# Q projection by Strassen's seven products in a transformer layer on one NeuronCore, with the stages reordered through DRAM

## The reference

```python
    x = x + xattn(layernorm(x), ctx, ctx, mask, Wq, Wk, Wv, Wo)
    x = x + ffn(layernorm(x), W_base, b_base, W_router, A, B)
# xattn: x and ctx are (16, 128, 1024); 32 query heads, 8 key/value heads, d = 128
    q = rope((query @ Wq).reshape(b, t, 32, 128));  k = rope((key @ Wk).reshape(b, t, 8, 128))
    v = (value @ Wv).reshape(b, t, 8, 128)
    logits = 30.0 * tanh(q k^T * 0.0883883 / 30.0), masked, then softmax
    return (weights @ v).reshape(b, t, 32 * 128) @ Wo
# ffn: 8 experts, top 2, rank 16
    base = xf @ W_base.T + b_base
    w = softmax of the top 2 router logits, spread over the 8 experts
    lora = einsum('ter,te,eor->to', einsum('td,erd->ter', xf, A), w, B) * 2
```

## Time and profile before

| | before |
|---|---|
| median of 3 runs | 2381.96 us (2380.62 to 2385.32) |
| span of the profiled execution | 2386.6 us |
| busy: PE, DVE, ACT, POOL | 2275.9, 1897.6, 928.1, 1286.0 us |
| matmuls | 9793 |
| moved by DMA | 258.35 MB, mean 108 GB/s |

### The profile page before, as it was taken

How to read it: one execution, slowest core, us unless ns; L and a number is a source line. 1 busy time by engine, 2 the same in 40 slices (tenths; PEclk the granted TensorE clock), 3 DMA queues, 4 the chain that set the end, 5 groups by cost and what they waited for, 6 DMA issues and landing times.

```text
span 2386.6 us, 26853 instructions
## 1 busy us (share of the span) xinstructions
PE 2275.9 (95%) x9793; PEld 1856.3 (78%) x9793; DVE 1897.6 (80%) x1954; ACT 928.1 (39%) x1306; POOL 1286.0 (54%) x720
## 2 busy tenths in 40 slices
PE   8999999999999899999989999998999999888999
PEld 6887878788887678888777888777778887777777
DVE  7436384787889898888998788899888789988992
ACT  3323334343453334334433434444333444333341
POOL 4235454456676445558654445855555476634441
PEclk9999999999999999999999999999999999999999
DMA  7545533232222242222224223222323322133331
GB/s 254 173 155 204 175 119 123 80 93 94 89 97 80 80 159 82 94 96 92 89 80 159 88 89 93 84 83 68 94 88 101 97 80 97 62 124 121 128 102 65
DMA packets 92482, 258.35 MB, mean 108 GB/s; under 512 B 9152, under 2 KB 25664, under 8 KB 92352
## 3 DMA queue, kind: packets, MB, share of 16 engines
q1 hardware_dynamic: 92352, 256.63, 33.0%
HBM read 227.24 MB, written 29.36 MB: 108 GB/s over the span
## 4 chain that ended last, share of the span: by engine, by line
PE 56%; DVE 24%; POOL 10%; issue 8%; ACT 2%; DMA 0%; DVEq 0%; SPq 0%; POOLq 0%; ACTq 0%
PE ps L450 18%; PE ps L451 18%; PE ps L452 18%; DVE AN L752 5%; POOL Rl L270 3%; DVE D L595 3%; POOL t L506 2%; POOL ql L270 2%; DVE Rl L270 2%; DVE L L537 2%; DVE t L503 2%; DVE t L501 1%; DVE Y L788 1%; DVE t L500 1%; POOL D L593 1%
## 5 line engine op out<-in xcount | busy, mean ns | idle before, releaser
L270 POOL TENSOR_TENSOR Rl<-raw,Rh 128x1024 fp32r<-128x1024 f32 x219 | 548.3, 2504 | 607.6 <-ACT Rh L267 606.3
L267 ACT ACTIVATE Rh<-raw 128x1024 fp32r<-128x1024 f32 x360 | 380.0, 1056 | 466.9 <-PE ps L452 457.7
L450 PE MATMUL ps<-Xh,Rh 128*128 128x512 f32 x1296 | 511.5, 395 | 13.3 <-DVE Xl L270 8.1
L450 PE MATMUL ps<-Ah,Rh 128*128 128x512 f32 x1296 | 509.8, 393 | 9.0 <-DVE Al L270 4.8
L451 PE MATMUL ps<-Xl,Rh 128*128 128x512 f32 x1296 | 509.5, 393 | 0.0
L452 PE MATMUL ps<-Xh,Rl 128*128 128x512 f32 x1296 | 508.9, 393 | 0.0
L451 PE MATMUL ps<-Al,Rh 128*128 128x512 f32 x1296 | 508.1, 392 | 0.0
L452 PE MATMUL ps<-Ah,Rl 128*128 128x512 f32 x1296 | 508.1, 392 | 0.0
L752 DVE RECIPROCAL AN<-ps 128x512 f32<-128x512 f32 x128 | 429.0, 3352 | 15.6 <-PE ps L748 12.4
L506 POOL TENSOR_TENSOR t<-t,t 128x512 f32<-128x512 f32 x160 | 251.0, 1569 | 195.4 <-DVE t L503 195.4
L270 DVE TENSOR_TENSOR Rl<-raw,Rh 128x1024 fp32r<-128x1024 f32 x141 | 220.3, 1565 | 101.6 <-ACT Rh L267 100.1
(11 more groups left out here) (139 smaller groups left out, 2960.2 us busy)
## 6 DMA issues: line engine op xcount, KB each, us to landing
raw<-gran SPq DMA_DIRECT2D x361, 512.0 KB, 3.5
raw<-ctxT SPq DMA_DIRECT2D x16, 512.0 KB, 4.3
kD<-t SPq DMA_DIRECT2D x32, 256.0 KB, 3.2
kraw<-kD SPq DMA_DIRECT2D x32, 256.0 KB, 2.6
vD<-st SPq DMA_DIRECT2D x32, 256.0 KB, 2.3
vraw<-vD SPq DMA_DIRECT2D x32, 256.0 KB, 3.2
Y<-xT SPq DMA_DIRECT2D x16, 512.0 KB, 6.6
out<-Y SPq DMA_DIRECT2D x16, 512.0 KB, 2.6
```

Source lines behind the costliest of these rows:

```text
L267: return put("act", waits, lambda e: e.activation(dst, src, ACT.Copy), cn("act_" + name), cost)
L270: return put(eng, waits, lambda e: e.tensor_tensor(dst, src, f(hidst), ALU.subtract), cn(eng + "_" + name), cost)
L450: put("pe", waits, lambda e: e.matmul(pe_out, lh, rh, start=first, stop=False), None, cost)
```

## The change

The work is laid out anew in four stages, with the intermediate results in DRAM.

1. K and V, two chunks at a time, so that each weight granule is loaded and split once for two chunks (48 loads of 512 KB for K, V and context, where there were 80). K and V are stored split, so they are not split again in each group. At the same time x is normalized: the statistics are taken from a second, token-major copy `xN` with BN_STATS (`x_stats`, L519) and spread to 128 x 512 tiles by eight plain fp32 matmuls (`x_spread`, L557). `x_blocks` (L577) forms the seven Strassen combinations of the four quadrants (two k halves by two chunks), splits them, and stores them in DRAM: 2 x 7 blocks of 2 MB.
2. Q: 32 quads of four output tiles (`q_quad`, L716). Each is seven products of 12 matmuls, where it was eight, with four additions for the weight combinations (`quad_weights`, L689), five DVE additions on PSUM, one ACT copy, and rope (`rotate`, L455), six DVE operations for two tiles. Q is stored in DRAM.
3. Attention and O: the S and PV pieces of a group stand among the O jobs of the group two before. The numerators are copied out by ACT, the four denominators of a group are put in one bank by means of a selector, and DVE takes one reciprocal per group (L853). It goes to DRAM (`rD`), comes back as four broadcast tiles `RB`, and multiplies the numerators from SBUF. The second layernorm (`ln2`, L917) reads x1 from DRAM and stores its split result there.
4. The feed-forward part for the four chunks, from DRAM.

The list schedule has new costs, and items that may go to either DVE or POOL ("flex"). Each engine now counts on one semaphore, where each kind of its operations had one.

```diff
-    COST = {"pe": 216, "act": 520, "dve": 600, "pool": 1230, "sp": 60}
-    SEEN, DMA_SEEN, DMA_NS_PER_KB = 90, 2100, 3.1
+    COST = {"pe": 227, "act": 630, "dve": 670, "pool": 1480, "sp": 60, "flex": 660}
+    ENGINES = ("pe", "act", "dve", "pool", "sp")
+    SEEN, DMA_SEEN, DMA_NS_PER_KB, SLOW, BACKLOG = 90, 2100, 3.6, 2.2, 3
...
+            if e == "dve":
+                mine = mine + ready["flex"]
+            elif e == "pool" and not mine and len(ready["dve"]) + len(ready["flex"]) > self.BACKLOG:
+                mine = sorted(ready["flex"], key=lambda r: r[:2])[self.BACKLOG - 1:]
...
+                m1 = tt("flex", t1, b12, b11, ALU.subtract, [n11, n12] + tt_free[0], "xb")
+                m3 = tt("flex", t3, b22, b12, ALU.subtract, [n22, n12] + tt_free[2], "xb")
+                m2 = tt("flex", t2, b22, t1, ALU.subtract, [n22, m1] + tt_free[1], "xb")
+                m4 = tt("flex", t4, b21, t2, ALU.subtract, [n21, m2] + tt_free[3], "xb")
+                blocks = [(b11, n11), (t2, m2), (b21, n21), (t3, m3), (t1, m1), (t4, m4), (b22, n22)]
...
+                    d = dma(XcD[cp, n, :, k], f(xst[s][:, :, :]), [h, l], f"d_xs{s}", 512)
...
+                got.append(dma(f(Xq[n][:, :, :, :]), XcD[cp, n], x_free[n] + Xc_store[cp, n], f"d_xq{n}", 2048))
...
+            m = product(0, b0, True, fr[0])
+            s1 = put("act", [m] + qp_free[par], lambda e: e.activation(r0, b0, ACT.Copy), cn("act_post"))
+            m = product(1, b1, True, fr[1])
+            u2 = tt("dve", r2, b1, r0, ALU.add, [m, s1] + qp_free[par], c)
+            m11 = product(2, b0, False, [s1])
+            m = product(3, b1, False, [u2])
+            u3 = tt("dve", r1, b1, r0, ALU.add, [m, s1] + qp_free[par], c)
+            m = product(4, b2, True, fr[2])
+            b3 = ps[6 + par][:, :]
+            c22 = tt("dve", b3, b2, r1, ALU.add, [m, u3] + fr[3], c)
+            m = product(5, b1, False, [u3])
+            c21 = tt("dve", b1, b1, r0, ALU.add, [m, u2, u3], c)
+            m = product(6, b2, False, [c22])
+            c12 = tt("dve", b2, b2, r2, ALU.add, [m, u2], c)
...
+            r = put("dve", [md] + rt_free, lambda e: e.reciprocal(rT[:, :], Tb[:, :]), cn("dve_o"), 3350)
+            tb_free[0] = [r]
+            st = dma(rD[i], rT[0:P:32, :], [r] + rd_free[i], f"d_rs{i}", 8)
+            rt_free[:] = [st]
+            ld = [dma(RB[:, x, :], bc(rD[i, x:x + 1, :], [P, T]), [st] + rb_free, f"d_rb{x}", 256) for x in range(4)]
...
+                o = tt("flex", AN[s][:, :], AN[s][:, :], RB[:, x, :], ALU.mult, [ld[x], an_marks[gi, x]], "an")
...
+                at_ = t - (8 * (gi - 2) + 3)
+                if at_ in (0, 2, 4, 6):
+                    att_s(gi, at_ // 2)
+                if at_ in (2, 4, 6, 8):
+                    att_pv(gi, at_ // 2 - 1)
+                    if at_ == 8 and gi + 2 < len(groups):
+                        att_load(gi + 2)
```

More of the change, by code:

```diff
@@ L105, in start @@
                 end, done = now + self.COST["sp"], dma_free + self.DMA_SEEN
+            elif it.engine == "flex" or e == "pool":
+                took = it.cost * (self.SLOW if it.engine == "flex" and e == "pool" else 1)
+                end = shared = max(now, shared) + took
+                done = end + self.SEEN
             else:
@@ L108, in start @@
                 done = end + self.SEEN
+            if it.engine == "flex" and it.counter is not None:
+                it.counter = it.counter[e]
             seq += 1
@@ L227, in program @@
[L227 to L239, removed]
@@ L247, in program @@
+        oh = here("oh", [P, 2, 4, 8], F32, 20.75)
+        wt = here("wt", [P, 4, 8], F32, 21)
+        ps = [ctx.enter_context(nc.psum_tensor(f"ps{i}", [P, 512], F32)) for i in range(8)]
         counters = {}
         def cn(name, step=1):
+            name = name if step > 1 else name.split("_")[0]
             if name not in counters:
@@ new lines, in step, with three @@
+        def step(job, evac, bg=1):
+            for _ in range(bg):
+                if background:
+                    t = background.pop(0)
+                    if t:
+                        t()
+            r = job()
+            last_job[0] = r[1]
+            flush()
+            pending.append(lambda: evac(r))
+        def three(pe_out, lh, ll, rh, rl, first, last, waits, mark=None, more=False):
+            put("pe", waits, lambda e: e.matmul(pe_out, lh, rh, start=first, stop=False, skip_group_check=more))
+            put("pe", [], lambda e: e.matmul(pe_out, lh, rl, start=False, stop=False, skip_group_check=more))
+            return put("pe", [], lambda e: e.matmul(pe_out, ll, rh, start=False, stop=last, skip_group_check=more), mark)
@@ L479, in job @@
                 for k in range(KC):
[L480 to L485 removed]
+                    rh, rl = KW.tiles(w + k // 2, k % 2, width=T)
@@ L647, in job, with o_job @@
+        rd_free = [[], []]
+        def o_job(gi, w, n):
+            par = gi % 2
             def job():
                 b, waits = bank()
[L649 to L658 removed]
@@ L765, in o_job @@
[L765 to L776 removed]
+                s = w % RING
@@ new lines, in f_job, with job @@
+        def f_job(w, c, fm, router=False, last=True):
+            def job():
+                b, waits = bank()
+                X = F2[c % 2]
+                for k in range(KC):
+                    lh, ll = OW.tiles(w, k)
+                    wait = (OW.marks[w] + waits if k == 0 else []) + [fm[k]]
+                    mark = cn("pe_job") if k == KC - 1 else None
+                    if router:
+                        put("pe", wait, lambda e, lh=lh, k=k: e.matmul(ps[b][:, :], lh, X[:, k, 0, :], start=k == 0, stop=False))
+                        m = put("pe", [], lambda e, lh=lh, k=k: e.matmul(ps[b][:, :], lh, X[:, k, 1, :], start=False, stop=k == KC - 1), mark)
+                    else:
+                        m = three(ps[b][:, :], lh, ll, X[:, k, 0, :], X[:, k, 1, :], k == 0, last and k == KC - 1, wait, mark)
+                OW.used(w, m)
+                return b, m
+            return job
```

1357 lines of the change are left out of this document (705 added, 652 removed).

## The result

The changed kernel takes **2415.06 us** (median of 4 runs, 2414.1 to 2419.83) against 2381.29 for the kernel before (median of 4 runs): a ratio of **1.0146** [1.0126, 1.0166]. It is slower by 1.5%, where 2.9% less was forecast. TensorE has 4% less work (a floor of 2135 us for 2221) and loses 277 us against it where it lost 166.

A forecast was written before the change was run, and what follows sets the result against it. The kernel was taken as bound by PE, but not by PE alone. A floor of 2135 us plus stage losses 36, 12, 10, 23, 20, 68 and 15 gave a 2319 us span, so 2314 us (2.9% less), range 2250 to 2390.

The forecast's parts named there:

- The floor and Q: All matmuls: floor of 2135 us; Q's 32 quads stay bound by PE at 19.05 us each, losing 10 us.
- would make the prediction wrong: Stated sign of failure: DVE's starts not 0.60 us apart on PSUM sources with both sides in PSUM, or added losses overlapping.
- Start and the second pair of chunks: First matmul at about 31 us, loss 36; replacing seven 2 MB Q blocks loses 19, with a slow restart 23.
- K, V and the change to Q: K and V stage: DVE not the bound, DMA's 120 MB just fits at 330 GB/s; 12 us of waits.
- Rival D: K and V bound by DMA at 257 GB/s: 78 us more, time 2392; chance 0.13.
- Q to attention: Change of stage: first scores, reciprocal, store and load at 2.6 us each, products stand uncovered; loss 20 us.
- Attention and O: Attention stage: DVE has 905 of 939 us, so PE loses 6.5%, 61 us, making 68 above the floor.
- The stretch 700 to 800: Stretch of the kernel before with DVE busy 93 us, lost 10%; taken as the model for DVE's 96% in attention.
- Rival C: Attention: the denominators' trip through DRAM holds up DVE; slower than before at two landings of about 5.5; time 2425, chance 0.13.
- The interference: Attention: POOL takes about 115 operations and adds 0.8 us to each overlapping DVE operation, half of them overlapping.
- The feed-forward part: Last stage: 1024 matmuls, DVE light except for one layernorm; loss 10 us, and 5 at the end.

The follow-up runs named there:

- run 7: Changed kernel with the second pair's first K granule loaded and split ahead of the last four context blocks: 2405.18 us.
- Runs 1 to 3: Against the changed kernel: 1, no scaling by denominators, 2353.31 us; 2, score and value jobs two output jobs earlier, 2378.65; 3, four earlier, seven AN buffers, 2355.65.
- run 6: Changed kernel with none of the shared elementwise work given to GpSimd, VectorE taking it all: 2373.58 us, ratio 0.9968 to the kernel before.
- run 8: Changed kernel with four staging buffers for V in place of two, and the last layernorm's sums later in TensorE's order: 2388.97 us.
- runs 9 and 11: 9: changed kernel with score and value jobs three earlier, seven AN buffers, edits of runs 6, 7, 8: 2324.49 us; 11: 9 with other layernorms' sums later: 2321.27.
- run 4: Changed kernel with the denominators' store and four broadcast loads issued by ScalarE in a DMA queue of their own: 2463.83 us, ratio 1.034.

## Why the prediction was wrong

*The floor and Q were right.* 2135 us of matmuls at 0.227 each; 443 matmuls in 100 us of Q while VectorE is 92% busy. Reckoned loss 10, measured none outside the change of blocks. What "would make the prediction wrong", a start distance of VectorE other than 0.60 us, did not occur: it is 0.60 for the sums with both sides in PSUM.

*Start and the second pair of chunks were a little too dear:* 31 us for 36 (first matmul at 29.1, reckoned 31), 12 for 23. The 19 in that term should have been 17 by its own figures, 50 less 33.

*K, V and the change to Q failed:* 12 reckoned, 53 measured. The step was to divide the bytes by the bandwidth and find that they fit. They did, but in a ring of four load buffers the context blocks went ahead of the granule that PE needed next (half of that pause, run 7), and two V buffers waited for stores queued behind 2 MB loads: 9.3 us from issue to landing where the median is 4.7. Both are waits of one transfer for its place, and neither shows in a mean. Rival D had the place right and the cause wrong, since the stretches moved 307 and 288 GB/s at shares of 0.88 and 0.78, the start even 387, where D had at most 257, and an order alone gave back 10 us. What holds PE in the rest of the first pause is open.

*Q to attention:* 20 reckoned, 36 measured. I priced the store at 2.6 us "the least landing of a 256 KB load"; it took 13.2, and the loads 4.5. In all groups between the first and the last it was 1.7 to 4.9 us from the issue of the store to that of the loads (median 2.5), so the price was right for a steady trip and wrong for the one behind twelve loads. These 10.6 us are most of the 16 that were missing here.

*Attention and O is the largest miss:* 68 above the floor reckoned, 104 in the 950 us of it measured. The step that failed is "DVE has 905 of 939 us ... I take 6.5%". That prices a throughput. VectorE was busy 842 of 950 us (89%), less than reckoned, and PE lost more. (The stretch 700 to 800 that stood for the 96% had lost 10% by busy time, but 63 of 440 matmuls, 14%.) It waited for the length of a trip that ends after the output job that needs it. Rival C named the trip and "two landings of about 5.5", and the load came near it (4.7 us), the store did not (median 2.5), but C put the damage at VectorE's head, idle for `RB`: that is 16.5 us in 22 waits. The wait that counts is PE's, for the last of four products and four splits behind it, and it needs no 5.5: a trip of 20.7 us against a distance of 18.7 is enough. I never laid the trip's sum against the distance from the last score job to the first output job that reads it, in PE's own order. Runs 1 to 3 show it: 2.2 of 58 us left without the trip, and with room for four jobs 59 us less with the trip whole.

*The interference was priced at its mean.* 0.8 us for half of 115 overlapping operations is 46 us; measured are (972 - 686) x 116 + (1225 - 682) x 95 + (727 - 682) x 77 ns = 88 us, nearly all in AN and Al. The price held (0.70 and 0.84 us for one of them), the number did not: 114 ran beside GpSimd in all, about twice the 57. And I had spread it over VectorE's queue, where it falls on the end of the trips (run 6).

*The feed-forward part:* 15 reckoned, 35 measured at 2100 to 2200 and none after, by the place of one layernorm product (16 us, run 8) and the last trip (14.4 us, with a store of 13.5).

So the losses reckoned as 184 were 277, and the 86 us by which the floor fell went into 111 us of new losses. Of the 93 us too little, about 41 are K and V, 16 the change to the attention, 36 the attention and 20 the end, less 16 at the start and the second pair and 10 in Q; the rest lies outside these stretches. That the best kernel's span, 2315 us, is near the 2319 reckoned confirms nothing: its losses are as large as reckoned, but in other places, 44 us of them in the prologue of the attention.

Not settled: what sets the prologue of the attention, where the kernels of runs 9 and 11 lose 40 and 44 us from 1000 to 1150 us and the changed one 36; the wait of 9.4 us at 400 us that is left in run 8; and by which way ScalarE's issues cost the 49 us of run 4. I did not try a second `Y2`, for which I found no room beside `AN`, nor one reciprocal per block again.

## What to carry to other kernels

Where a change sends a result on a longer way, lay the sum of the way's steps against the distance, in the waiting engine's own order, between the work that starts it and the work that asks for it; the busy shares say nothing on that, and a few places more in the order can give back what the way costs (59 us here, where 18.7 us of distance stood against 20.7 of trip). At each change of stage, walk the queue and the buffers ring by ring to the first transfer that the new stage needs, for a fit of bytes by bandwidth hides pauses of 20 us. And an engine that takes over work when another has a backlog does so at the critical moment: check there, not on average, what it slows down. When the way has room, look again: the same help can then be worth keeping.

## What the runs showed of the hardware that I had not expected

- A store of 8 KB took 13.2 us from issue to landing behind twelve larger transfers, and the same one on ScalarE's queue at most 8.5, while the broadcast loads on that queue took 6.0 us (median) for 4.7.
- In the changed kernel GpSimd's help was worth almost nothing as throughput: VectorE did 151 more operations for 15 us more of busy time when GpSimd was idle. Single operations of 0.68 us had been stretched to as much as 2.9. With room for the trip that help was worth some 14 us from the attention on.
- PE's granted clock was low around the long pauses: 0.76 to 0.79 in the two stretches of 50 us that hold a wait of 20 to 25 us, 0.99 from 250 to 400 us between them, where PE was busy 149.98 of 150 us.
